# Self attention of a decoder layer: the probabilities of a head divided by their sums on ScalarE instead of GpSimd

## The chip, the cores and the metric
The kernel is one program on one core of a Trainium2 chip. The metric is the device time of one execution in microseconds, as the median of several. Engine names in the rows: PE is TensorE's matmul side and PEld its weight loads, DVE is VectorE, ACT is ScalarE, POOL is GpSimd, SP is SyncE.

## The reference
The program computes two decoder layers for 16 batches of 256 tokens of width 512, everything in float32. Its first step, the one that is changed here, is causal self attention with rotary positions:

```python
q = einsum('bsd,hdk->bshk', layernorm(x), W_Q) + b_Q      # 16 heads of 64; k and v alike
q, k = rotary(q), rotary(k)
scores = where(causal, einsum('bqhd,bkhd->bhqk', q, k) / 8, -inf)
pattern = softmax(scores, axis=-1)
x = x + einsum('bqhd,hdm->bqm', einsum('bhqk,bkhd->bqhd', pattern, v), W_O) + b_O
```

After it come a cross attention (`cross0`), an expert layer, a normalised linear attention (`norm`), a second cross attention (`cross1`) and an fp8 linear layer. Each is a phase of its own with a barrier behind it.

## The kernel before
`attention_phase` serves the self attention (`rotary` is true, tiles are called `self_...`) and both cross attentions (`rotary` is false, `cross_...`). A phase walks over 16 batches, and within a batch over 16 slots, one for each head. The five engines each run the same loop (`body(b, first, last)`) with their own part of every slot, and meet at semaphores. Each engine does its work in the order in which the code issues it, so the first thing that waits holds up all that is behind it on this engine.

For a head h of the self attention the steps are, in order:

1. TensorE, slot h (heads come in pairs, so in even slots): `scores` of h and h+1 into two of four banks, then the causal mask is added (L509, L516).
2. VectorE, `maxima` (L754): the negative row maxima of both heads of the pair. Four reductions of 128x128 and 128x256, one of each for a head.
3. ScalarE, `exps` in slot h (L617): exponentials from the bank into `prob`, two instructions (128x128 and 128x256), each with a reading of the accumulator that gives the row sums.
4. VectorE, `sums_inverse` in slot h+1 (L761): `rsum`, the reciprocals of the sums.
5. GpSimd (L404): `prob` times `rsum` in place, two instructions. It then raises `norm_ok`.
6. TensorE, `prob_transposes` in slot h+2 (L528): waits for `norm_ok` and transposes the probabilities into the bank `T`, which VectorE (even heads, L767) or ScalarE (odd heads, L625) copies to `probT`.
7. TensorE, `times_v` in slot h+4 (L544), into the bank `Z`; VectorE copies it to `zT` one slot later (`heads_done`, L776).

Between these steps stand the projections, by a fixed plan of slots (`PLAN`). Each goes through one of two banks `A`, used in turn: the use u waits until u-1 uses are free (`bank_for`).

- slots 0, 2, 4, 6, 8, 10, 12: `Q`, the transposes of the turned q and k of the next pair of heads (L456). ScalarE copies the q half (`self_QT`, L605), then VectorE the k half (`self_KT`, L699), which frees the bank
- slots 0 and 1, and 8 to 11, 14 and 15: `P`, projections of q and k, 12 matmuls each (L70 to L72). VectorE turns them (L827, L828), and GpSimd adds the two parts and the turned bias (L382, L384)
- slots 3 and 4: `O`, the output projection of the batch before, one half of the tokens each (L472). It needs all eight `zT` of that batch, the last of which VectorE writes in slot 3
- slots 5 and 6, and 12 and 13: `V`, projections of v, copied by VectorE (L694)
- slot 7: `X`, twice: transposes of the next batch's normalised x (L442); ScalarE rounds them to `self_xTh` (L598), VectorE takes the rest as `self_xTl` (L683)

`P` of slots 8 to 11, 14 and 15 belongs to the next batch. The first of them, in slot 8, and `Q` of slot 14 wait on TensorE until every earlier use of the two banks is free:

```python
if key in (("+", "P", 0, 0, 0), ("+", "Q", 0)):
    pe.wait_ge(a_free, u)
```

The orders of VectorE and ScalarE within a slot, which the argument needs:

- VectorE: `zT` of an earlier pair (odd slots), `maxima` of the pair (even slots), the copy of `probT` (even slots), `rsum` of head i-1, then the extras of the plan (`self_KT`, the turning, `self_xTl`, the copy of v)
- ScalarE: the copy of `probT` (odd slots), `exps` of head i, then the extras (`self_QT`, `self_xTh`)

Of the kernel before, what the change touches and what calls it, by code (L numbers as in the profile page):

```python
# [22 lines left out]
ALU = mybir.AluOpType  # L23
ACT = mybir.ActivationFunctionType
AX = mybir.AxisListType

P = 128
# [3 lines left out]
T = S // P  # L31
H = 16
# [43 lines left out]
def after(eng, sem, value):  # L76

    if not isinstance(value, int) or value > 0:
        eng.wait_ge(sem, value)


def over_rotated(eng, n, body, tail):


    body(0, True, False)
    if n > 2:
        with eng.Fori(1, n - 1) as b:
            body(b, False, False)
    body(n - 1, False, True)
    tail(n)  # L90
# [34 lines left out]
def attention_phase(nc, name, n_batch, x_in, x_out, consts, wq, wk, wv, wo,  # L125
                    d_head, causal, rotary, ctx=None, bq=None, bk=None, bv=None, bo=None, rope=None):
# [20 lines left out]
    KQ = [P * (t + 1) if causal else S for t in range(T)]  # L147
    SOFF = [sum(KQ[:t]) for t in range(T)]
# [4 lines left out]
    NP = 4 if rotary else 8  # L153
# [64 lines left out]
    with Phase(nc, name) as ph:  # L218
# [22 lines left out]
        rsum = ph.sb("rsum", [P, H, T])  # L241
        prob = ph.sb("prob", [P, NP, SW])
# [49 lines left out]
        rsum_ok = ph.sem("rsum_ok")  # L292
        norm_ok = ph.sem("norm_ok")
# [70 lines left out]
        @block.gpsimd  # L364
        def _(pool):
            def rstds(n):
                pool.wait_ge(ln, 7 * n + 5)
                pool.tensor_tensor(rstd[:, :], rstd[:, :], minus_half[:, :], ALU.pow).then_inc(ln_pow, 1)

            pool.memset(minus_half[:, :], -0.5).then_inc(pool_const, 1)  # L370
            pool.wait_ge(pool_const, 1)
            rstds(0)
            pool.wait_ge(const_in, 16 * N_CONST)
            if rotary:
                pool.wait_ge(rb_ok, 3 * 2 * T * CH)

            def turned(key, u, seq):

                _, which, c, t = key
                dst = (q_t, k_t)[which][:, t, c * 512:(c + 1) * 512]  # L380
                pool.wait_ge(a_free, u + 1)
                pool.tensor_tensor(dst, dst, turn[:, t % 2, :], ALU.add).then_inc(rot, 1)  # L382
                pool.wait_ge(rot, 2 * seq + 1)
                pool.tensor_tensor(dst, dst, rb[:, which, t, c * 512:(c + 1) * 512], ALU.add).then_inc(rot, 1)  # L384

            for key in BEFORE:
                if key[0] == "P":
                    turned(key, N_W + BEFORE.index(key), [k for k in BEFORE if k[0] == "P"].index(key))

            def body(b, first, last):  # L390
                seq = 0
                for i in range(H):
                    for key in PLAN[i]:
                        ahead = key[0] == "+"
                        if key[ahead] == "P" and not (ahead and last):
                            turned(key[ahead:], uses.at(key, b, first, last), P_BEFORE + b * P_PER + seq)
                            seq += 1
                    if i == STATS_AT and not last:
                        rstds(b + 1)

                    pool.wait_ge(rsum_ok, b * H + i + 1)
                    for t in range(T):
                        pr = prob[:, i % NP, SOFF[t]:SOFF[t] + KQ[t]]
                        ins = pool.tensor_tensor(pr, pr, rsum[:, i, t:t + 1].to_broadcast([P, KQ[t]]), ALU.mult)  # L404
                    ins.then_inc(norm_ok, 1)
                if bo is not None:

                    pool.wait_ge(res_in, b * 16 + 16)
                    for t in range(T):
                        pool.tensor_tensor(res[:, t, :], res[:, t, :], bo_r[:, :], ALU.add).then_inc(res_b, 1)  # L410
            over_rotated(pool, n_batch, body, lambda b: None)
# [166 lines left out]
        @block.scalar  # L578
        def _(act):
            if rotary:  # L580
                for i in range(N_STAGE):
                    w = (wqs, wks, wvs)[i // 2]
                    act.wait_ge(w_in[i % 3], 16 * KD * (i // 3 + 1))
                    act.activation(w[0][:, :, (i % 2) * 512:(i % 2 + 1) * 512],
                                   stage[i % 3][:, :, :].rearrange("p t n -> p (t n)").rearrange("p (k n) -> p k n", k=KD), ACT.Copy).then_inc(w_hi, 1)
            else:
                for u in range(N_W):
                    act.wait_ge(a_full, u + 1)
                    act.activation((wqs, wks, wvs, wos)[u // KD][0][:, u % KD, :], A[u % 2][:, :], ACT.Copy).then_inc(a_hi, 1)
            if not rotary and bq is not None:  # L590
                act.wait_ge(zeroed, 1)
            act.wait_ge(const_in, 16 * N_CONST)

            def extra(key, u, bank, n):
                if key[0] in "XC":
                    act.wait_ge(a_full, u + 1)
                    j = key[1]
                    act.activation((xT if key[0] == "X" else cT)[0][:, 2 * j:2 * j + 2, :].rearrange("p k n -> p (k n)"),  # L598
                                   A[bank][:, :], ACT.Copy).then_inc(a_hi, 1)
                elif key[0] == "Q":  # L600
                    g = key[1]
                    act.wait_ge(a_full, u + 1)
                    after(act, s_full, n * H + HPT * (g + 1 - n_qt))
                    if rotary or bq is None:
                        act.activation(QT[:, g % n_qt, :], A[bank][:, 0:S], ACT.Copy, scale=SCALE).then_inc(a_hi, 1)  # L605
                    else:

                        act.activation(QT[:, g % n_qt, :], A[bank][:, 0:S], ACT.Identity, bias=bq_c[:, g:g + 1], scale=SCALE).then_inc(a_hi, 1)

            for j, key in enumerate(BEFORE):  # L610
                extra(key, N_W + j, (N_W + j) % 2, 0)

            def exps(b, h):
                act.wait_ge(max_ok, b * H + h + 1)
                after(act, t_full, b * H + h - NP + 1)
                for t in range(T):
                    ins = act.activation(prob[:, h % NP, SOFF[t]:SOFF[t] + KQ[t]], SC[h % 4][:, SOFF[t]:SOFF[t] + KQ[t]], ACT.Exp,  # L617
                                         bias=neg_max[:, h, t:t + 1], scale=1.0, accum_out=sums[:, h, t:t + 1])
                ins.then_inc(exp_ok, 1)

            def probs_odd(b, h):
                if h % 2:
                    act.wait_ge(t_full, b * H + h + 1)
                    after(act, pv_ok, b * H + h - NPT + 1)
                    act.activation(probT[:, h % NPT, :], TP[:, 0:SW], ACT.Copy).then_inc(pt_odd, 1)  # L625

            def heads_hi(b, h, first, last):
                if not rotary and h % G == 0:
                    g = (h % H) // G
                    act.wait_ge(pv_ok, b * H + h + G)  # L630
                    if h == 0 and not first:
                        act.wait_ge(a_full, uses.at(("O", 1), b, first, last) + 1)
                    if bv is None:
                        act.activation(zTs[0][:, g, :], Z[:, 0:S], ACT.Copy).then_inc(z_hi, 1)
                    else:

                        act.activation(zTs[0][:, g, :], Z[:, 0:S], ACT.Identity, bias=bv_c[:, g:g + 1]).then_inc(z_hi, 1)

            def body(b, first, last):
                for i in range(H):  # L640
                    if not (first and i < Z_LAG):
                        heads_hi(b, i - Z_LAG, first, last)
                    if not (first and i < T_LAG):
                        probs_odd(b, i - T_LAG)
                    for j in EXP_AT[i % G]:
                        exps(b, i - i % G + j)
                    for key in PLAN[i]:
                        ahead = key[0] == "+"
                        if not (ahead and last) and key[ahead] in "QXC":
                            extra(key[ahead:], uses.at(key, b, first, last), uses.bank(key, b, first, last), b + 1 if ahead else b)  # L650

            def tail(b):
                for i in range(Z_LAG):
                    heads_hi(b, i - Z_LAG, False, False)
                    if i < T_LAG:
                        probs_odd(b, i - T_LAG)

            over_rotated(act, n_batch, body, tail)

# [1082 lines left out]
```

## Time and profile before

| | |
|---|---|
| median of 3 runs | 4279.06 us (4275.65 to 4281.77) |
| profiled execution | 4277.14 us, its span 4275.4 us |
| self attention | about 57 to 1400 us of the span |
| granted clock of TensorE over the span | 0.913 |
| busy over the span | PE 82%, PEld 57%, DVE 46%, POOL 33%, ACT 29% |
| POOL instructions of L404 on `self_prob` | 512, two for each of 256 heads |

How to read it: the span runs from the first to the last instruction of one profiled execution. The busy share of an engine is a mean over phases with different limits. A granted clock of 1.00 is TensorE at 2.4 GHz, 0.50 is 1.2 GHz, and a value between is a mean over the stretch. A row of busy time by stretch has, in order: the stretch in us from the span's start and its length; then for PE, PEld, DVE, ACT and POOL the busy time in us with the count of instructions; then the granted clock, the busy share of the DMA engines and GB/s. What stands in square brackets behind an instruction is the idle time of its engine before it and what ended that.

### The profile page before, as it was taken

The page shows a single profiled execution, that of the slowest core. Times are in us where ns is not written, and L with a number is a line of the kernel's source. Part 1 is how long each engine was busy: PE and PEld are TensorE (multiplying, and loading weights), DVE is VectorE, ACT ScalarE, POOL GpSimd, SP SyncE. Part 2 cuts the span into 40 slices and gives each one's busy share as a digit, 9 for nine tenths or more (in the row PEclk, how much of TensorE's full clock was granted, in tenths as well). Part 3 has the DMA queues.
Part 4 walks back from the last instruction along what each step waited for, and adds up shares of the span by engine and source line. Part 5 has one row for each costly group of instructions (what it writes and reads, how often), then busy time and mean ns, then how long its engine had stood idle before and what let it go on. Part 6 is the DMA issues. An engine that isn't in the chain of part 4 may idle for free. (4 is left out here: it accounts for less than half of the span.)

```text
span 4275.4 us, 70717 instructions
## 1 busy us (share of the span) xinstructions
PE 3514.4 (82%) x23116; PEld 2419.5 (57%) x23116; DVE 1965.1 (46%) x4934; ACT 1255.4 (29%) x4320; POOL 1421.7 (33%) x2092
## 2 busy tenths in 40 slices
PE   4999999999998799999857666655999799999955
PEld 3665666666565577777626111111777577777732
DVE  5444444444443455555450000001566466666657
ACT  2222222222222345555410000000111255555521
POOL 2444445444444133333310000000222145455437
PEclk9999999999998799999985877777999899999976
DMA  5000000000000211111166999997111211111113
GB/s 118 16 20 15 25 15 20 25 15 20 15 25 11 81 40 59 40 58 42 37 218 242 425 429 426 426 429 282 54 67 67 78 40 49 46 52 39 49 53 133
DMA packets 158787, 459.15 MB, mean 107 GB/s; under 512 B 47393, under 2 KB 51873, under 8 KB 138209
## 3 DMA queue, kind: packets, MB, share of 16 engines
q1 hardware_dynamic: 150272, 445.72, 27.3%
q10 hardware_dynamic: 8448, 12.59, 0.9%
q8 instruction: 36, 0.59, 0.1%
q14 instruction: 31, 0.25, 0.0%
HBM read 402.17 MB, written 56.10 MB: 107 GB/s over the span
## 5 line engine op out<-in xcount | busy, mean ns | idle before, releaser
L404 POOL TENSOR_TENSOR cross_prob<-cross_prob,cross_rsum 128x256 f32<-128x256 f32 (+1 forms) x1024 | 559.8, 572 | 760.9 <-DVE cross_rsum L761 760.9
L617 ACT ACTIVATE cross_prob<-cross_S,cross_neg_max 128x256 f32<-128x256 f32 (+1 forms) x1024 | 440.8, 464 | 1.4 <-DVE cross_neg_max L754 1.4
L617 ACT ACTIVATE self_prob<-self_S,self_neg_max 128x128 f32<-128x128 f32 (+1 forms) x512 | 210.2, 418 | 569.6 <-DVE self_neg_max L754 569.6
L404 POOL TENSOR_TENSOR self_prob<-self_prob,self_rsum 128x128 f32<-128x128 f32 (+1 forms) x512 | 247.8, 507 | 383.7 <-DVE self_rsum L761 383.3
L528 PE MATMUL cross_T<-cross_ident,cross_prob 128*128 128x128 f32 x1792 | 290.0, 279 | 85.6 <-ACT cross_probT L625 76.7
L528 PEld LDWEIGHTS cross_T<-cross_ident,cross_prob 128*128 128x128 f32 x1792 | 205.4, 142 | 147.4 <-issue 85.7
L1171 PE MATMUL experts_H<-moe_w,experts_tok 128*32 128x512 f32 x1024 | 167.8, 815 | 141.7 <-DMA moe_b<-in_L_ffn_w 137.2
L625 ACT ACTIVATE cross_probT<-cross_T 128x384 f32<-128x384 f32 (+1 forms) x256 | 139.7, 546 | 423.4 <-PE cross_T L528 423.4
L472 PE MATMUL self_A<-self_wo_f,self_zT 128*128 128x512 f32 x512 | 254.3, 656 | 0.6 <-DVE self_zT L776 0.6
L617 ACT ACTIVATION_READ_ACCUMULATOR cross_prob<-cross_S,cross_neg_max 128x1 f32 x1024 | 230.5, 225 | 0.0
L1189 PE MATMUL experts_O<-moe_w,experts_hidT 128*32 128x512 f32 x1024 | 170.1, 825 | 51.7 <-DMA moe_w<-in_L_ffn_w 45.9
L1311 POOL MEMSET norm_minus_half<- 128x2 f32 x1 | 0.1, 104 | 638.5 <-POOLq L53 638.5
L1231 DVE COPY experts_hidT<-experts_T 128x512 f32<-128x512 f32 x32 | 22.1, 691 | 381.9 <-PE experts_T L1182 381.9
L1171 PEld LDWEIGHTS experts_H<-moe_w,experts_tok 128*32 128x32 f32 x1024 | 44.5, 143 | 264.1 <-issue 257.7
L528 PE MATMUL self_T<-self_ident,self_prob 128*128 128x128 f32 x768 | 137.2, 290 | 59.2 <-POOL self_prob L404 58.1
L754 DVE TENSOR_REDUCE self_neg_max<-self_S 128x1 f32<-128x128 f32 (+1 forms) x512 | 147.1, 349 | 74.4 <-PE self_S L516 74.4
L756 DVE TENSOR_REDUCE cross_neg_max<-cross_S 128x2 f32<-128x512 f32 x256 | 158.9, 683 | 43.4 <-PE cross_S L509 43.3
L472 PEld LDWEIGHTS self_A<-self_wo_f,self_zT 128*128 128x128 f32 x512 | 107.0, 215 | 126.9 <-issue 125.9
L625 ACT ACTIVATE self_probT<-self_T 128x384 f32<-128x384 f32 x128 | 62.8, 490 | 344.9 <-PE self_T L528 344.9
L754 DVE TENSOR_REDUCE cross_neg_max<-cross_S 128x1 f32<-128x128 f32 (+1 forms) x512 | 141.3, 348 | 42.9 <-PE cross_S L516 42.9
L767 DVE COPY cross_probT<-cross_T 128x384 f32<-128x384 f32 (+1 forms) x256 | 156.1, 610 | 9.4 <-PE cross_T L528 9.4
L70 PE MATMUL cross_A<-cross_xTh,cross_wqh 128*128 128x256 f32 x512 | 156.1, 305 | 2.8 <-DVE cross_cTl L683 2.8
(270 smaller groups left out, 8896.3 us busy)
## 6 DMA issues: line engine op xcount, KB each, us to landing
moe_w<-in_L_ffn_w SPq DMA_DIRECT2D x64, 4096.0 KB, 34.9
cross_x_t<-x SPq DMA_DIRECT2D x32, 512.0 KB, 3.9
cross_c_t<-in_ctx SPq DMA_DIRECT2D x32, 512.0 KB, 4.8
cross_res<-x SPq DMA_DIRECT2D x32, 512.0 KB, 3.6
x<-cross_res SPq DMA_DIRECT2D x32, 512.0 KB, 2.8
self_x_t<-in_x SPq DMA_DIRECT2D x16, 512.0 KB, 3.6
self_res<-in_x SPq DMA_DIRECT2D x16, 512.0 KB, 3.6
x<-self_res SPq DMA_DIRECT2D x16, 512.0 KB, 2.8
```

Source lines behind the costliest of these rows:

```text
L70: pe.matmul(out, ah, bh, start=first, stop=False)
L404: ins = pool.tensor_tensor(pr, pr, rsum[:, i, t:t + 1].to_broadcast([P, KQ[t]]), ALU.mult)
L472: mm = pe.matmul(A[bank][:, :], zT[:, k, t * P:(t + 1) * P], wo_f[:, k, :], start=(k == 0), stop=(k == NT - 1))
L528: mm = pe.transpose(TP[:, o:o + P], prob[:, h % NP, SOFF[t] + k * P:SOFF[t] + (k + 1) * P], ident[:, :])
L617: ins = act.activation(prob[:, h % NP, SOFF[t]:SOFF[t] + KQ[t]], SC[h % 4][:, SOFF[t]:SOFF[t] + KQ[t]], ACT.Exp, bias=neg_max[:, h, t:t + ...
L625: act.activation(probT[:, h % NPT, :], TP[:, 0:SW], ACT.Copy).then_inc(pt_odd, 1)
L754: ins = dve.tensor_reduce(neg_max[:, h, t:t + 1], SC[h % 4][:, SOFF[t]:SOFF[t] + KQ[t]], AX.X, ALU.max, negate=True)
L756: ins = dve.tensor_reduce(neg_max[:, h, :], SC[h % 4][:, :].rearrange("p (t k) -> p t k", t=T), AX.X, ALU.max, negate=True)
L767: dve.tensor_copy(probT[:, h % NPT, :], TP[:, 0:SW]).then_inc(pt_even, 1)
L1171: pe.matmul(HP[s][32 * n:32 * n + 32, :], tok[:, s, k, :], w1_s[s][:, k, n * 512:(n + 1) * 512], start=(k == 0), stop=False, tile_position ...
L1189: mm = pe.matmul(OP[s][32 * n:32 * n + 32, :], hidT[:, s, q, 32 * n:32 * n + 32], w2_s[s][:, n, q, :], start=(q == 0), stop=(q == NQ - 1), ...
L1231: dve.tensor_copy(hidT[:, s, :, :].rearrange("p q n -> p (q n)"), TP[s][:, :]).then_inc(ht_ok, 1)
```

## The change
In the self attention the two multiplications by `rsum` go from GpSimd to ScalarE, as a copy with a scale for each row. ScalarE does them for head i-1 in slot i, after the exponentials of head i and ahead of the slot's extras. The cross attentions keep theirs on GpSimd. Nothing else is edited.

```diff
-                    pool.wait_ge(rsum_ok, b * H + i + 1)
-                    for t in range(T):
-                        pr = prob[:, i % NP, SOFF[t]:SOFF[t] + KQ[t]]
-                        ins = pool.tensor_tensor(pr, pr, rsum[:, i, t:t + 1].to_broadcast([P, KQ[t]]), ALU.mult)
-                    ins.then_inc(norm_ok, 1)
+                    if not rotary:
+                        pool.wait_ge(rsum_ok, b * H + i + 1)
+                        for t in range(T):
+                            pr = prob[:, i % NP, SOFF[t]:SOFF[t] + KQ[t]]
+                            ins = pool.tensor_tensor(pr, pr, rsum[:, i, t:t + 1].to_broadcast([P, KQ[t]]), ALU.mult)
+                        ins.then_inc(norm_ok, 1)
...
+            def normalised(b, h):
+
+                act.wait_ge(rsum_ok, b * H + h + 1)
+                for t in range(T):
+                    pr = prob[:, h % NP, SOFF[t]:SOFF[t] + KQ[t]]
+                    ins = act.activation(pr, pr, ACT.Copy, scale=rsum[:, h % H, t:t + 1])
+                ins.then_inc(norm_ok, 1)
...
                     for j in EXP_AT[i % G]:
                         exps(b, i - i % G + j)
+                    if rotary and not (first and i < 1):
+                        normalised(b, i - 1)
                     for key in PLAN[i]:
...
                     if i < T_LAG:
                         probs_odd(b, i - T_LAG)
+                    if rotary and i < 1:
+                        normalised(b, i - 1)
```

## Rows read from the trace of the kernel before

**Rows 1.** Busy time by stretch, the self attention (columns: see above).

```profile
57.00:1400.00 1343.00, 1228.37 (x6762) 834.02 (x6761) 616.49 (x1653) 332.93 (x1310) 617.85 (x815) 0.96 0.05 18
```

**Rows 2.** Waits by total, 200 to 1100 us: total, times, longest.

```profile
PE self_T L528 <- POOL self_prob L404: 33.6, 22, 2.6
...
PE self_A L456 <- DVE self_turn L828: 18.4, 11, 1.8
PE self_A L70 <- DVE self_KT L699: 16.1, 10, 1.6
...
PEld self_T L528 <- POOL self_prob L404: 10.1, 27, 0.7
```

**Rows 3.** Timeline of TensorE, slots 2 to 4: start, duration, instruction.

```profile
656.15 0.40 PE L516 MATMUL self_S<-self_mask_b,self_ident_b 128*128 128x128 bf16 x4
657.02 0.55 PE L528 MATMUL self_T<-self_ident,self_prob 128*128 128x128 f32 x3 [0.46 <-POOL self_prob L404]
...
657.62 0.38 PE L456 MATMUL self_A<-self_ident,self_k_t 128*128 128x128 f32 x2
660.59 0.54 PE L528 MATMUL self_T<-self_ident,self_prob 128*128 128x128 f32 x3 [2.59 <-POOL self_prob L404]
660.97 8.73 PE L472 MATMUL self_A<-self_wo_f,self_zT 128*128 128x512 f32 x16
...
672.29 7.03 PE L472 MATMUL self_A<-self_wo_f,self_zT 128*128 128x512 f32 x16
```

**Rows 4.** Timeline of GpSimd, slots 2 and 3.

```profile
659.49 1.90 POOL L404 TENSOR_TENSOR self_prob<-self_prob,self_rsum 128x128 f32<-128x128 f32 x4
```

**Rows 5.** The same columns in the wait of slot 3 and behind it.

```profile
657.00:660.50 3.50, 0.98 (x7) 0.75 (x7) 2.14 (x8) 1.21 (x5) 3.42 (x5) 1.00 0.00 0
...
662.00:664.00 2.00, 2.00 (x4) 0.72 (x3) 0.00 (x0) 0.46 (x3) 0.00 (x0) 0.50 0.00 0
```

**Rows 6.** The same columns after the waits of slots 8 and 14.

```profile
200.00:1100.00 900.00, 831.48 (x4605) 563.96 (x4604) 421.54 (x1132) 225.77 (x890) 422.30 (x556) 0.97 0.05 19
611.30:621.00 9.70, 9.65 (x57) 7.35 (x58) 4.63 (x12) 2.23 (x10) 5.29 (x7) 1.00 0.00 0
642.10:652.00 9.90, 9.89 (x63) 7.83 (x64) 4.70 (x13) 2.95 (x12) 7.88 (x9) 1.00 0.16 53
```

**Rows 7.** ScalarE's own durations: this op's nearest relatives.

```profile
L617 ACT ACTIVATE self_prob<-self_S,self_neg_max 128x256 f32<-128x256 f32 x174 | 81.9, 471 | 0.0
...
L617 ACT ACTIVATE self_prob<-self_S,self_neg_max 128x128 f32<-128x128 f32 x174 | 63.5, 365 | 394.7 <-DVE self_neg_max L754 394.7
...
L605 ACT ACTIVATE self_QT<-self_A 128x256 f32<-128x256 f32 x87 | 33.2, 381 | 45.0 <-PE self_A L456 45.0
```

**Rows 8.** By tile `top_pr`, duration min/median/max in ns: an ACTIVATE from SBUF to SBUF.

```profile
L1074 ACT ACTIVATE top_pr<-top_pr,top_nm x4: 491/492/507, 2233.1 to 2234.6; 128x256 f32<-128x256 f32 x4
```

**Rows 9.** Timeline of ScalarE, end of slot 7.

```profile
606.97 0.21 ACT L617 ACTIVATION_READ_ACCUMULATOR self_prob<-self_S,self_neg_max 128x1 f32 x1
607.07 1.09 ACT L598 ACTIVATE self_xTh<-self_A 128x512 fp32r<-128x512 f32 x2
```

**Rows 10.** Timeline of VectorE, slots 7 and 8.

```profile
607.70 1.29 DVE L683 TENSOR_TENSOR self_xTl<-self_A,self_xTh 128x512 fp32r<-128x512 f32 x2 [0.99 <-ACT self_xTh L598]
608.91 1.14 DVE L754 TENSOR_REDUCE self_neg_max<-self_S 128x1 f32<-128x128 f32 x4
...
610.43 0.15 DVE L761 RECIPROCAL self_rsum<-self_sums 128x2 f32<-128x2 f32 x1
610.77 0.42 DVE L699 COPY self_KT<-self_A 128x256 f32<-128x256 f32 x1 [0.19 <-ACT self_QT L605]
```

**Rows 11.** TensorE in slot 8, at the first projection for the next batch.

```profile
611.33 0.49 PE L70 MATMUL self_A<-self_wqh,self_xTh 128*128 128x512 f32 x1 [1.61 <-DVE self_KT L699]
```

**Rows 12.** Timeline of VectorE, slots 2 and 3.

```profile
656.48 1.15 DVE L754 TENSOR_REDUCE self_neg_max<-self_S 128x1 f32<-128x128 f32 x4 [0.49 <-PE self_S L516]
...
658.45 0.42 DVE L699 COPY self_KT<-self_A 128x256 f32<-128x256 f32 x1
658.79 0.47 DVE L776 TENSOR_SCALAR self_zT<-self_Z,self_bv_c 128x256 f32<-128x256 f32 x1
```

## The prediction, made before the changed kernel was run

> **What bounds the kernel now.** I first read the busy time by stretch, to find which engine fills the self attention. TensorE is busy for 1228.37 of 1343 us, ScalarE for 332.93, GpSimd for 617.85 [rows 1]. So the phase is bound by TensorE, and what another engine does costs time only where TensorE stands still for it, or where its clock falls.
>
> Then the waits by total over 11 of the 16 batches [rows 2]. TensorE's transposes waited 33.6 us for GpSimd's product, 3.05 us a batch. Two other waits stand beside it: 18.4 us for the turning (1.66 us a batch, slot 14), and 16.1 us for `self_KT` (slot 8, 1.61 us each time [rows 11]).
>
> The timeline shows where the 3.05 us are. Slot 2 waits 0.46 us and slot 3 2.59 us [rows 3]: GpSimd still adds up the q and k of the projections, and gets to the products of heads 1 and 2 only at 659.49 [rows 4], though the sums of head 1 were there earlier. Behind the wait of slot 3 the granted clock is 0.50 in 662 to 664 us, the lower of the two levels, 1.2 GHz [rows 5]. What TensorE did before: 0.98 us of work in 3.5 us [rows 5]. The 16 matmuls of `O` that fall into it take 8.73 us, and the same 16 one slot later 7.03 us [rows 3]: 1.70 us lost a visit. Behind the waits of 1.61 us (slot 8) and 1.66 us (slot 14) the clock stayed at 1.00, 2.4 GHz [rows 6]. Over the 11 batches it was 0.97 [rows 6]; 3% of 900 us is 27 us, 2.4 us a batch, about that one visit, sometimes a longer one.
>
> **What the change removes.** 512 GpSimd products go. GpSimd was on the path only in the waits named: 3.05 us a batch at TensorE, and part of the 10.1 us that weight loads waited [rows 2]. That is 0.92 us a batch, most of it the same wait of slot 2; the rest, in later slots, I take as 0.3 us, between nothing and 0.46. The projections' additions on GpSimd come a little earlier; nobody waits for them for long.
>
> **What it adds.** Two ScalarE instructions a head, SBUF to SBUF, with a scale read for each row. No row shows this one. The nearest: an ACTIVATE of 128x256 in SBUF with a bias for each row takes 0.492 us [rows 8]; from a PSUM bank 0.471, and its 128x128 form 0.365 [rows 7]. So 0.49 and 0.39 us. Neighbours overlap by 0.11 us (606.97 + 0.21 against 607.07 [rows 9]), say 0.10. The pair takes 0.78 us, and what is behind it starts 0.68 us later. Bounds: without the row operand 0.381 for the large one [rows 7], pair about 0.65; at no overlap 0.88.
>
> The Trainium skill (VectorE: DVE Perf Modes, section "The TRN2 errata — SBUF-src ops pay a fixed extra latency per instruction") speaks against moving this work here: ScalarE pays 224 cycles of fixed cost from SBUF and 172 from PSUM, an estimated 0.04 us more for each instruction. Here 0.492 against 0.471 shows half of that [rows 7, 8]; by the page the sum below would be 1 to 2 us longer.
>
> ScalarE is idle most of the time, so by busy share 512 more instructions are free. By order they are not: they stand ahead of the slot's extras. I follow each place where an extra is waited for.
>
> Slot 7: the pair of head 6 stands between the exponentials of head 7 and the two roundings of x, which start at 607.07 [rows 9] as soon as ScalarE is free. They come 0.68 us later, and with them the two subtractions of VectorE, behind which stand the maxima of slot 8, at 608.91 back to back [rows 10]. They start at 609.59.
>
> Slot 8: `rsum` comes 1.52 us behind the start of the maxima (610.43 - 608.91 [rows 10]), since VectorE copies a transposed head between them. Until now `self_QT` did not wait for it. Now it waits for the pair, and the pair for `rsum`: 609.59 + 1.52 + 0.15 for `rsum` + 0.08 for the signal = 611.34, then 0.68 to `self_QT` (612.02), 0.41 to `self_KT` (612.43), and 0.56 from the start of `self_KT` to TensorE, as before (611.33 - 610.77 [rows 10, 11]). TensorE starts the projection at 612.99 where it was 611.33: **+1.66 us**, a wait of 3.27 us where it was 1.61.
>
> Slots 2 and 3: the maxima start at 656.48, after a wait for TensorE, so nothing earlier moves them [rows 12]. `rsum` of head 1 is done at 658.15, the pair runs 658.23 to 659.01, and head 1's transposes start at 659.07, not 660.59 [rows 3]. But `self_KT` also moves, from 658.45 to 658.23 + 0.68 + 0.41 = 659.32, and the last `zT` is behind it on VectorE, 0.34 us later: 659.66 to 660.13 [rows 12]. The output projection needs it. It starts at 660.23, not 660.97 [rows 3]: **-0.74 us**, though the transposes come 1.5 us earlier.
>
> Other even slots: `self_KT` comes 1.0 us later too (1.86 us behind the start of the maxima before [rows 10], 2.84 now). What TensorE does next there is a projection of 12 matmuls, about 3 us, so it is hidden; with the least to spare in slot 6. If that cover were gone, the two transposes of x would start late.
>
> **Sum.** A batch: +1.66 - 0.74 - 0.3 = +0.62 us; 15 batches, +9.3 us. The first and last batch have few projections, and there heads wait for GpSimd's products as well: some -2 us. Bounds of the pair: it counts twice in slot 8 and once in slot 3, so 0.13 us less gives 6 us less, 0.1 us more 5 us more.
>
> **The clock.** It now costs about 2.2 to 2.4 us a batch. The wait of slot 3 is cut into 1.5 us (657.62 + 0.38 less the shift of slot 2, to 659.07) and 0.8 us, which is less than what brought the lower level down and more than what did not; I expect it in a part of the batches. The wait of slot 8 becomes longer than the 2.59 us that brought it in this row's batch; I expect it there in most. One visit costs 1.7 us. So the loss moves and stays about as large; I put -1 us for it. 4277.1 + 9.3 - 2 - 1 = 4283.4 for the profiled execution, which stands 1.9 us below the median: 4285.3, say **4286 us**.
>
> **Rivals.**
>
> - The forecast: the stall moves from slot 3 to slot 8, the clock's loss with it. Own range 4274 to 4300. Chance 0.62.
> - Slower by more: the lower level comes in slot 8 and in slots 2 and 3 as well. For: both waits lie above the 1.66 us that were harmless [rows 2, 6]. Against: the second is broken up. 15 visits of 1.7 us or a little more are 26 to 30 us: 4313. It decides if the two shorter waits of slots 2 and 3 count together as the one long wait did. Chance 0.15.
> - Faster: the lower level comes in neither place. For: no single wait of slots 2 and 3 is now over 1.7 us. Against: slot 8's 3.3 us. Then 15 x 2.3 = 34 us come back against 9.3 - 2: 4252. Chance 0.15.
> - Much faster: the pair is covered in slots 7 and 8, and all of the 3.05 + 0.3 us and the clock come back: 15 x 5.6 = 84 us, 4195. Against: ScalarE's roundings start back to back and the maxima too [rows 9, 10]. Chance 0.05.
> - The rest 0.03.
>
> **How the numbers follow.** Within 0.2% is 8.6 us, about what this kernel's measurement can tell. The forecast lies at +7, so of its 0.62 I give 0.35 to no change, 0.25 to slower, 0.02 to faster. With 0.15 slower, 0.15 + 0.05 faster and the rest: faster 0.22, same 0.37, slower 0.41. The range 4256 to 4312 takes in the forecast's own and goes to both clock rivals.
>
> **What would show it.** In the waits: TensorE's wait of slot 8 for `self_KT` at 3.2 us instead of 1.61; transposes of slot 3 that wait 1.4 us for ScalarE, then 0.8 us of the output projection for `zT`; no wait for GpSimd left in this phase. The pair at 0.39 and 0.49 us. The clock at 0.50 behind slot 8. The prediction is wrong in its order if slot 7's maxima chain does not move, and in its size if the clock does not follow the waits as said.

## The result, and the profile after

The changed kernel takes 4299.55 us in the median, the one before 4275.65 us beside it: ratio 1.0054, 95% interval 1.0032 to 1.0077. It is slower, by 24 us or 0.5%. In the profiled executions the difference is 27.6 us (4304.70 against 4277.14), and all of it arises in the self attention. The last instruction of that phase that VectorE does ends 27.5 us later. First the kernel before, then the changed one:

```profile
1403.30 0.69 DVE L709 TENSOR_TENSOR self_res<-self_A,self_res 128x512 f32<-128x512 f32 x1 [6.17 <-PE self_A L472]
```

```profile
1430.82 0.69 DVE L722 TENSOR_TENSOR self_res<-self_A,self_res 128x512 f32<-128x512 f32 x1 [6.18 <-PE self_A L473]
```

Busy time by stretch of the changed kernel, the self attention (columns as in [rows 1]):

```profile
57.00:1400.00 1343.00, 1226.57 (x6686) 845.26 (x6685) 608.94 (x1635) 518.34 (x1794) 378.71 (x303) 0.94 0.05 18
```

GpSimd has lost 239 us of work against [rows 1], ScalarE has gained 185. Neither bounds the phase. The granted clock went from 0.96 to 0.94. The waits of the changed kernel by total, 200 to 1100 us, beside [rows 2]:

```profile
PE self_A L70 <- DVE self_KT L712: 34.9, 11, 3.2
...
PE self_A L457 <- DVE self_turn L841: 18.3, 11, 1.7
PE self_T L529 <- ACT self_prob L633: 18.1, 10, 1.8
...
PE self_A L473 <- DVE self_zT L789: 4.9, 10, 0.6
```

TensorE waits for GpSimd no more in this phase. The wait of slot 8 has doubled, from 1.61 to 3.17 us a batch. In slots 2 and 3 there are now 1.81 us for ScalarE and then up to 0.6 us for `zT`, where there were 0.46 and 2.59 us. Timeline of TensorE, slots 2 and 3 of two batches:

```profile
416.42 0.49 PE L529 MATMUL self_T<-self_ident,self_prob 128*128 128x128 f32 x3
...
419.16 0.54 PE L529 MATMUL self_T<-self_ident,self_prob 128*128 128x128 f32 x3 [1.81 <-ACT self_prob L633]
420.28 7.13 PE L473 MATMUL self_A<-self_wo_f,self_zT 128*128 128x512 f32 x16 [0.58 <-DVE self_zT L789]
...
504.27 8.37 PE L473 MATMUL self_A<-self_wo_f,self_zT 128*128 128x512 f32 x16 [0.40 <-DVE self_zT L789]
```

VectorE in the same slots, beside [rows 12]:

```profile
416.51 1.15 DVE L767 TENSOR_REDUCE self_neg_max<-self_S 128x1 f32<-128x128 f32 x4 [0.49 <-PE self_S L517]
...
419.33 0.42 DVE L712 COPY self_KT<-self_A 128x256 f32<-128x256 f32 x1 [1.13 <-ACT self_QT L606]
419.67 0.47 DVE L789 TENSOR_SCALAR self_zT<-self_Z,self_bv_c 128x256 f32<-128x256 f32 x1
```

From the start of the maxima to the output projection are 3.77 us (420.28 - 416.51); before they were 4.49 (660.97 - 656.48 [rows 3, 12]). That is 0.72 us won, though the transposes of head 1 alone come 1.46 us earlier (2.65 us behind the maxima, not 4.11). `self_KT` starts 2.82 us behind the maxima, not 1.97, and holds up the last `zT`.

Slot 8. ScalarE at the end of slot 7, then VectorE, then TensorE:

```profile
447.17 0.21 ACT L618 ACTIVATION_READ_ACCUMULATOR self_prob<-self_S,self_neg_max 128x1 f32 x1
447.26 0.80 ACT L633 ACTIVATE self_prob<-self_prob,self_rsum 128x128 f32<-128x128 f32 x2
447.95 1.08 ACT L599 ACTIVATE self_xTh<-self_A 128x512 fp32r<-128x512 f32 x2
```

```profile
449.78 1.14 DVE L767 TENSOR_REDUCE self_neg_max<-self_S 128x1 f32<-128x128 f32 x4
...
451.31 0.15 DVE L774 RECIPROCAL self_rsum<-self_sums 128x2 f32<-128x2 f32 x1
452.59 0.42 DVE L712 COPY self_KT<-self_A 128x256 f32<-128x256 f32 x1 [1.13 <-ACT self_QT L606]
```

```profile
453.15 0.79 PE L70 MATMUL self_A<-self_wqh,self_xTh 128*128 128x512 f32 x1 [3.17 <-DVE self_KT L712]
...
538.38 0.79 PE L70 MATMUL self_A<-self_wqh,self_xTh 128*128 128x512 f32 x1 [3.17 <-DVE self_KT L712]
```

The pair stands between the accumulator's reading and the roundings of x, which follow 0.69 us after its start. `self_KT` starts 2.81 us behind the maxima, not 1.86 [rows 10]. The first matmul behind the wait takes 0.79 us, not 0.49 [rows 11]: the clock is down. Busy time by stretch of the changed kernel, behind slot 3 of one batch, behind slot 8, and ahead of slot 3 of the next batch:

```profile
504.00:506.50 2.50, 2.23 (x3) 1.18 (x4) 0.21 (x2) 1.89 (x7) 0.00 (x0) 0.50 0.00 0
538.50:544.00 5.50, 5.50 (x14) 4.23 (x15) 0.00 (x0) 0.00 (x0) 0.00 (x0) 0.50 0.00 0
571.00:588.00 17.00, 15.22 (x100) 11.47 (x100) 9.19 (x25) 7.75 (x28) 12.74 (x10) 1.00 0.09 31
```

The lower level, 1.2 GHz, comes twice in this batch, and behind slot 8 it lasts more than 5.5 us. In what follows, one such stretch is called a visit; in all the traces here a visit in the steady batches lasts either about 3.4 or about 6.8 us. Last, ScalarE's own durations by form, for the instruction that no row of before showed:

```profile
L633 ACT ACTIVATE self_prob<-self_prob,self_rsum 128x256 f32<-128x256 f32 x170 | 85.0, 500 | 0.0
...
L633 ACT ACTIVATE self_prob<-self_prob,self_rsum 128x128 f32<-128x128 f32 x170 | 68.7, 404 | 17.7 <-DVE self_rsum L774 12.9
```

### The profile page after: what moved, and what is told of

The parts are those of the page before. It is cut to its first block and busy times, and to the rows that moved or that the text cites. A ratio compares the mean times of both kernels' runs of the same rounds, so it can differ in the third digit from the quotient of the medians.

```text
span 4302.9 us, 70507 instructions
## 1 busy us (share of the span) xinstructions
PE 3538.2 (82%) x23116; PEld 2442.2 (57%) x23116; DVE 1964.0 (46%) x4934; ACT 1449.2 (34%) x4832; POOL 1182.5 (27%) x1580
## 5 line engine op out<-in xcount | busy, mean ns | idle before, releaser
L382 POOL TENSOR_TENSOR self_q_t<-self_q_t,self_turn 128x512 f32<-128x512 f32 x64 | 81.7, 1277 | 718.4 <-DVE self_turn L841 718.3
L473 PE MATMUL self_A<-self_wo_f,self_zT 128*128 128x512 f32 x512 | 245.0, 634 | 8.0 <-DVE self_zT L789 8.0
L633 ACT ACTIVATE self_prob<-self_prob,self_rsum 128x128 f32<-128x128 f32 (+1 forms) x512 | 205.4, 452 | 27.6 <-DVE self_rsum L774 21.3
L70 PE MATMUL self_A<-self_wqh,self_xTh 128*128 128x512 f32 x256 | 123.4, 482 | 83.9 <-DVE self_KT L712 47.4
```

The costliest lines, as they stand in the source:

```text
L70: pe.matmul(out, ah, bh, start=first, stop=False)
L473: mm = pe.matmul(A[bank][:, :], zT[:, k, t * P:(t + 1) * P], wo_f[:, k, :], start=(k == 0), stop=(k == NT - 1))
L633: ins = act.activation(pr, pr, ACT.Copy, scale=rsum[:, h % H, t:t + 1])
```

## The experiments

All ratios are to the kernel before, with 95% intervals. The changed kernel stands at 1.0054.

**The division behind the extras, everywhere** (extras_first). "The division" is the pair of multiplications by `rsum`. In ScalarE's loop:

```diff
-                    if rotary and not (first and i < 1):
-                        normalised(b, i - 1)
                     for key in PLAN[i]:
...
+                    if rotary and not (first and i < 1):
+                        normalised(b, i - 1)
```

> The changed kernel, with ScalarE's division of head i-1 behind the slot's extras (self_QT, self_xTh) and no longer ahead of them; all else as changed. Theory A (order): the 512 instructions cost nothing in themselves, what they cost is that two chains stand behind them. So the wait of slot 8 goes from 3.17 us back to 1.61 us, head 1's transposes still start about 1.4 us earlier than before the change, and the output projection right behind them. Against the kernel before: -1.4 - 0.3 us a batch for the waits, and some 2 us a batch of clock if neither wait brings the lower level; 15 batches, about -55 us, ratio 0.987. Theory B (load): 512 more instructions (some 205 us busy) on ScalarE slow the chain of exponentials wherever they stand: the time stays within 0.3% of the changed kernel, ratio 1.003 to 1.008. Theory C (clock only): the changed kernel is slower since the clock falls more often; the waits do not matter by themselves: ratio about 1.00, with the clock up.

Ratio 0.9969 (0.9959 to 0.9979), 4262.49 us. Faster than both kernels, so theory B falls: the 512 instructions are still there. But it missed theory A's 0.987 widely and lies nearer to the 1.00 of theory C, the clock. Half of TensorE's busy time at the lower level in the self attention, an estimate of what that level costs, fell from 71 us in the changed kernel to 34 us, of 47 us between the two profiled executions. TensorE's waits by total show where it still stands:

```profile
PE self_T L529 <- ACT self_prob L633: 35.4, 22, 1.9
...
PE self_A L457 <- DVE self_turn L844: 18.3, 11, 1.7
...
PE self_A L70 <- DVE self_KT L715: 15.9, 11, 1.5
```

Slot 8 is back at 1.45 us. But TensorE now waits for ScalarE 22 times in this stretch, not 10 times. The second is in slot 15, behind the wait of slot 14. TensorE, then ScalarE:

```profile
468.63 0.43 PE L457 MATMUL self_A<-self_ident,self_q_t 128*128 128x128 f32 x2 [1.66 <-DVE self_turn L844]
468.90 0.38 PE L457 MATMUL self_A<-self_ident,self_k_t 128*128 128x128 f32 x2
470.61 0.90 PE L529 MATMUL self_T<-self_ident,self_prob 128*128 128x128 f32 x3 [1.33 <-ACT self_prob L633]
```

```profile
469.42 0.38 ACT L606 ACTIVATE self_QT<-self_A 128x256 f32<-128x256 f32 x1 [4.08 <-PE self_A L457]
469.70 0.79 ACT L633 ACTIVATE self_prob<-self_prob,self_rsum 128x128 f32<-128x128 f32 x2
```

In slot 14 ScalarE stood 4.08 us before `self_QT`, with the division of head 13 behind it. The transposes then take 0.90 us, not 0.50. Waits of 1.66 and 1.33 us with 0.65 us of work between them were followed by the lower level in all 14 batches that have them; 1.66 us alone was not, in any run.

**The same, but in slot 14 ahead of the extras** (behind_not14).

```diff
+                    late = i != 14
+                    if rotary and not late and not (first and i < 1):
+                        normalised(b, i - 1)
                     for key in PLAN[i]:
...
+                    if rotary and late and not (first and i < 1):
+                        normalised(b, i - 1)
```

> As extras_first, but in slot 14 the division stands ahead of the extras again. There the extra (self_QT of Q) waits for TensorE until late in the slot, and in extras_first the division of head 13 waited behind it and TensorE's transposes for 1.33 us. Theory A (order): that wait goes; slots 3, 8 and 14 each keep one wait of 1.4 to 1.9 us and none of them brings the lower level. Against the kernel before: -1.5 us a batch of waits, -2.2 us of clock, 15 batches: -55 us, ratio 0.987. Theory B (load of ScalarE): no more than extras_first, ratio 0.997.

Ratio 0.9878 (0.9861 to 0.9895), 4224.84 us, as expected. Slots 2 to 4 on TensorE; both halves of the output projection now take 7.03 us, with nothing between transposes and projection:

```profile
398.07 0.54 PE L529 MATMUL self_T<-self_ident,self_prob 128*128 128x128 f32 x3 [1.89 <-ACT self_prob L633]
398.45 7.03 PE L473 MATMUL self_A<-self_wo_f,self_zT 128*128 128x512 f32 x16
...
408.08 7.03 PE L473 MATMUL self_A<-self_wo_f,self_zT 128*128 128x512 f32 x16
```

**Slot 8's wait for `self_KT` taken away**, in the changed kernel (nowait_after), in the one before (nowait_before), and in the one just shown (behind_not14_nowait). The projection has its own bank, and the rest of x is in the uses that `bank_for` waits for.

```diff
-                        if key in (("+", "P", 0, 0, 0), ("+", "Q", 0)):
+                        if key in ((("+", "Q", 0),) if rotary else (("+", "P", 0, 0, 0), ("+", "Q", 0))):
                             pe.wait_ge(a_free, u)
```

> The changed kernel, in which the first projection for the next batch (slot 8) no longer waits until self_KT has freed its bank, but only for its own bank and for the rest of x. Theory A (the stall sits at this wait): 3.17 us a batch of waiting and the lower clock level behind it (6.8 us of it in most batches, 3.4 us lost) go; 15 batches x 6.5 us = -95 us against the changed kernel, ratio to the kernel before 0.98 to 0.985. Theory B (ScalarE's chain holds everything up): the wait comes back at the next thing that needs self_KT or head 7's transposes, and less than 1.5 us a batch is won, ratio 1.000 to 1.003.

> The kernel before the change, with the same wait of slot 8 taken away. 1.61 us a batch and no clock loss go: 15 batches, -24 us, ratio 0.9944, if the clock behind slot 3 stays as it was. Beside the same edit of the changed kernel it says what the change is worth where slot 8 does not stop TensorE: theory A wants the changed one then faster than this one by some 45 us (0.74 + 0.3 us a batch of waits and up to 2.2 us of clock); theory B wants it slower still.

> behind_not14 without slot 8's wait for self_KT. Theory A: another 1.5 us a batch of waiting, 15 batches, -22 us: ratio 0.982, some 15 us ahead of nowait_after. If ScalarE's load were the limit, no faster than nowait_after, 0.985.

The changed kernel falls to 0.9854 (0.9838 to 0.9870), 4214.12 us: 85 us less than with the wait, near the expected 95. The kernel before falls to 0.9960 (0.9945 to 0.9974), 4259.62 us, 16 us and not 24. Its granted clock is lower, 0.96 over 200 to 1100 us instead of 0.97 [rows 6]: the wait of slot 3 is the same, but every visit behind it now lasts 6.8 us, where most lasted 3.4 us.

```profile
200.00:1100.00 900.00, 847.37 (x4662) 573.66 (x4661) 425.86 (x1143) 229.86 (x901) 424.94 (x561) 0.96 0.05 19
```

So where slot 8 does not stop TensorE, the change is worth 45 us (4259.62 - 4214.12), just what theory A said: where the exposed chain is absent, moving the products from GpSimd to ScalarE is a gain. Most of it is clock. By the same estimate the lower level costs 57 us without the change and 23 us with it. The third kernel takes 4199.12 us, ratio 0.9816 (0.9797 to 0.9834), the fastest of all.

**The clock by itself.** Eight matmuls whose result is overwritten, ahead of TensorE's wait: in the changed kernel in slot 8 (fill8_after), in the kernel before in slot 3 (fill3_before). The edit in slot 8:

```diff
+                        if key == ("+", "P", 0, 0, 0) and rotary:
+                            bank_for(u)
+                            for _ in range(8):
+                                pe.matmul(A[uses.bank(key, b, first, last)][:, :], xT[0][:, 0, 0:P], wqs[0][:, 0, 0:512], start=True, stop=True)
```

> The changed kernel with 8 matmuls of 128x512 added, whose result is overwritten, between the transposes of slot 8 and its wait for self_KT (some 1.9 us of TensorE work in a wait of 3.17 us). They shorten no chain. Theory C (most of the loss beyond the waits is the clock): the granted clock stays at 1.00 behind slot 8, 3.4 us a batch come back, 15 batches, -50 us against the changed kernel, ratio to the kernel before about 0.993. If the time goes with the waits alone, nothing changes: ratio 1.005.

> The kernel before the change, with 8 matmuls of 128x512 added whose result is overwritten, on TensorE ahead of its wait for GpSimd in slot 3 (1.9 us of work in a wait of 2.59 us). No chain is shorter. Theory C (clock): the lower level behind slot 3 goes, 2.2 us a batch: -33 us, ratio 0.992. If the clock were not what those matmuls lose by, nothing changes: ratio 1.00.

The changed kernel: 0.9978 (0.9968 to 0.9987), 4264.15 us, 35 us less (32 by the two ratios), with 8 x 15 more matmuls. Expected were 50 us and a ratio of 0.993, so it fell short: the visits behind slot 8 are gone, but in slot 3, where nothing was filled, the lower level still comes in 8 of 14 batches. The added work takes 2.12 us, the projection still waits for `self_KT`, and its first matmul takes 0.50 us and no longer 0.79:

```profile
437.80 2.12 PE L567 MATMUL self_A<-self_wqh,self_xTh 128*128 128x512 f32 x8
440.95 0.50 PE L70 MATMUL self_A<-self_wqh,self_xTh 128*128 128x512 f32 x1 [1.03 <-DVE self_KT L716]
```

In the kernel before the added work takes 2.11 us. Its ratio is 0.9930 (0.9913 to 0.9947), 4245.49 us against 4276.73 us beside it, 31 us less. The output projection of slot 3 takes 7.03 us and not 8.73 [rows 3], and the clock over 200 to 1100 us is 1.00:

```profile
407.26 0.54 PE L528 MATMUL self_T<-self_ident,self_prob 128*128 128x128 f32 x3 [0.75 <-POOL self_prob L404]
407.64 7.03 PE L472 MATMUL self_A<-self_wo_f,self_zT 128*128 128x512 f32 x16
```

```profile
200.00:1100.00 900.00, 850.13 (x4817) 584.71 (x4815) 433.21 (x1161) 232.90 (x917) 433.58 (x570) 1.00 0.06 19
```

**The division behind the extras in one slot only**: 7, 8 or 2.

```diff
+                    late = i in (7,)
```

> The changed kernel with the division behind the extras in slot 7 alone. Theory A: of the 1.56 us by which the wait of slot 8 has grown, the pair of slot 7 is 0.68: the wait falls from 3.17 to 2.5 us, the rest stays. 15 batches x 0.68 = -10 us, and the clock may fall less often, up to 2 us a batch: between -10 and -40 us against the changed kernel, ratio 0.996 to 1.003. Rival: VectorE's copies, not the pair of slot 7, set the start of the maxima, and the wait stays 3.17 us, ratio 1.005.

> The changed kernel with the division behind the extras in slot 8 alone. Theory A: this is the other part of slot 8's grown wait, 1.56 - 0.77 (measured in slot7_behind) = 0.8 to 0.95 us: the wait falls from 3.17 to 2.2 to 2.4 us, and with it the longer visits to the lower level (6.8 us become 3.4, as in slot7_behind): ratio about 1.000. If the two parts did not add up, the wait would stay over 2.7 us.

> The changed kernel with the division behind the extras in slot 2 alone. Theory A: the output projection no longer waits 0.58 us for the last zT, the transposes ahead of it wait 0.1 us more: -0.5 us a batch, -7 us, with the stall of 3.17 us in slot 8 as in the changed kernel. With the 0.58 us gone, the clock no longer falls in slot 3 either, in half or more of the batches (in behind_not14 a single wait of 1.9 us rarely brought the lower level), 1.7 us a visit: ratio 0.997 to 1.003. Rival: another thing than self_KT holds the zT up, and the 0.58 us stay, ratio 1.005.

| division behind in | ratio | median us | wait of slot 8 | wait for `zT` |
|---|---|---|---|---|
| nowhere (changed kernel) | 1.0054 (1.0032 to 1.0077) | 4299.55 | 3.17 | up to 0.6 |
| slot 7 | 1.0008 (0.9999 to 1.0018) | 4277.93 | 2.40 | 0.58 |
| slot 8 | 0.9970 (0.9959 to 0.9980) | 4262.04 | 2.22 | 0.58 |
| slot 2 | 0.9970 (0.9958 to 0.9981) | 4264.11 | 3.17 | none |

The last two columns are in us. The two parts of slot 8's growth are 0.77 us (slot 7) and 0.95 us (slot 8). Together 1.72 us, more than the 1.56 us by which the wait had grown: with the division behind everywhere it is 1.45 us, less than the 1.61 us of before; why it is less stays open. Slot 8's edit did better than its expected 1.000, since the level also fell less often in slot 3, which that edit does not touch. The wait for `zT` goes with the pair of slot 2. Both rivals fall. The times, though, do not follow the waits: slot 2's edit takes 0.5 us a batch of waiting away (the transposes wait 1.89 us, not 1.81) and wins 35 us, 2.4 us a batch. The rest is clock. Busy time by stretch over 200 to 1100 us in slot2_behind, granted clock 0.98, then in the changed kernel, 0.95:

```profile
200.00:1100.00 900.00, 825.84 (x4663) 571.59 (x4662) 425.56 (x1144) 362.14 (x1254) 260.68 (x209) 0.98 0.06 19
```

```profile
200.00:1100.00 900.00, 825.23 (x4510) 568.78 (x4510) 411.27 (x1103) 349.63 (x1209) 260.04 (x208) 0.95 0.05 18
```

## Why the prediction came out as it did

The forecast was 4286 us, with 0.41 on slower, 0.37 on no change and 0.22 on faster. Measured: 4299.55 us, slower, inside the range of 4256 to 4312 and at the very end of the forecast's own 4274 to 4300; the profiled execution, 4304.70 us, lies beyond that. The order of the waits was understood, and slower was the likeliest of the three by a little. Most of the measured slowing, though, is a clock term that the sum had wrong; that the time still fell inside the range is owed to a width that took in the clock rivals.

- **That the stall moves from slot 3 to slot 8** was right, shown by the traces and by the kernels without slot 8's wait. The wait there was to be 3.27 us, and is 3.17. Its two parts were 0.68 and 0.98 us; undone one at a time they measure 0.77 and 0.95.
- **That slots 2 and 3 give back only 0.74 us** was right: 0.72. `self_KT` and with it the last `zT` hold the projection up, which slot2_behind confirms.
- **The pair at 0.78 us** measures 0.80, its parts 0.404 and 0.500 us, foreseen 0.39 and 0.49. The larger one stands 0.03 us above the exponential of the same shape out of PSUM, 0.471 us [rows 7]. For a source in SBUF, the Trainium skill (VectorE: DVE Perf Modes, section "The TRN2 errata — SBUF-src ops pay a fixed extra latency per instruction") gives 52 more fixed cycles, an estimated 0.04 us. The sign agrees; the two instructions here also differ in their function, so the 0.03 us is not the source's alone.
- **The cover in the other even slots** held: no further wait of TensorE appeared.
- **The clock term failed in size and sign.** I had put -1 us: the loss moves and stays as large. The waits account for +1.56 - 0.72 - 0.3 = +0.54 us a batch, 8 us in 15 batches, less the 2 us of the ends. The profiled difference is 27.6 us, so by this sum some 21 us are the clock. It may be all of it: the same estimate from the two traces gives 44 us before and 71 us after. The 0.3 us for later slots was never measured alone and would then be larger. The rival that had the lower level in both places (0.15, 4313 us) is what the trace shows: 0.50 behind slot 3 and behind slot 8 in one batch, and behind slot 8 for longer than one of the old visits. The filled waits price it: 31 us were lost to slot 3's wait before, and 35 us are lost to slot 8's wait now, with slot 3's on top.
- **The step under that term**: the prediction cut the wait of slot 3 into 1.5 and 0.8 us and expected the level there in a part of the batches only. The pieces are 1.81 and 0.58 us, and the level came in 12 of 14 batches. The first piece is longer because TensorE is done with slot 2 0.68 us earlier (0.84 us behind the start of the maxima, 417.35 - 416.51, not 1.52), and not only 0.46. So the first piece alone already lies above the 1.66 us that had been harmless.
- **The second, short wait is not shown to be the cause.** In 10 of the 12 batches it is shorter, 0.40 or 0.46 us, because the level had already fallen while the transposes ran, ahead of it. The stretch of the transposes at 503.16, before and behind the fall:

```profile
503.00:503.35 0.35, 0.19 (x2) 0.20 (x3) 0.02 (x1) 0.29 (x2) 0.00 (x0) 1.00 0.00 0
503.45:503.85 0.40, 0.40 (x3) 0.03 (x1) 0.40 (x2) 0.00 (x0) 0.00 (x0) 0.50 0.00 0
```

- **The same two waits without the lower level** stand in slot8_behind, where it came behind them in 1 of 14 batches:

```profile
653.42 0.55 PE L529 MATMUL self_T<-self_ident,self_prob 128*128 128x128 f32 x3 [1.80 <-ACT self_prob L633]
654.54 7.13 PE L473 MATMUL self_A<-self_wo_f,self_zT 128*128 128x512 f32 x16 [0.57 <-DVE self_zT L792]
```

- **What the runs leave open**: what, beside the waits, decides a batch. One undivided wait of 1.89 us was followed by the level in none of the 14 batches (extras_first and slot2_behind alike), in 4 (behind_not14) and in 6 (behind_not14_nowait).
- **The gain is real but was spent.** The same change is worth 45 us where slot 8 does not wait, and 52 us (4276.73 - 4224.84) once the extras go ahead of the division in every slot but 14.

## What to carry to other kernels

Work moved to an idle engine costs by its place in that engine's order: put it behind what others wait for and ahead of what itself waits long, slot by slot: the first rule alone won 13 us over the kernel before, and with slot 14 excepted 52 us. Before moving work, look for the one wait on TensorE that needs more than it must: with slot 8's wait gone the same edit gained 45 us, with it the edit lost 24. And do not price a TensorE wait by its length alone. Slot 14's 1.66 us cost no clock until 1.33 us followed 0.65 us of work later, and one and the same pair of waits in slot 3 brought the lower level in 12 of 14 batches of one kernel and in 1 of 14 of another.

## What the hardware showed that I had not expected

- The same waits, another clock. Waits of 1.61 and 1.66 us never brought the lower level, 2.59 and 3.17 us did in every batch. Between them it varied with the kernel: 1.81 us, 0.5 to 0.7 us of work and then up to 0.58 us brought it in 1 (slot8_behind), 5 (slot7_behind and nowait_after), 8 (fill8_after) and 12 (the changed kernel) of 14 batches.
- The visit's length varied as well. Behind the same 3.17 us in slot 8 it lasted 6.8 us in 12 of 14 batches of the changed kernel, and 3.4 us in all 14 of slot2_behind.
- Useless matmuls in a wait make the kernel faster: 8 of them a batch, 2.1 us of work in a wait, won 31 us and 35 us.
- Three kernels with different waits in slot 8 (1.45, 2.22 and 3.17 us) came out within 2.1 us of each other (4262.49, 4262.04 and 4264.11). Most of this is no riddle: TensorE's waits of a batch in slots 3, 8, 14 and 15 add up to 6.33, 6.26 and 6.72 us, and in nearly every batch each kernel has one visit, of 3.4 us. In all three the same instruction returns 81.9 us later in the next batch; in the changed kernel 85.2 us later (538.38 - 453.15). Why these distances are the ones that last was not tried and stays open.

The three in this order, extras_first, slot8_behind and slot2_behind, at slot 8 of two batches each:

```profile
438.33 0.49 PE L70 MATMUL self_A<-self_wqh,self_xTh 128*128 128x512 f32 x1 [1.44 <-DVE self_KT L715]
...
520.24 0.49 PE L70 MATMUL self_A<-self_wqh,self_xTh 128*128 128x512 f32 x1 [1.45 <-DVE self_KT L715]
```

```profile
440.71 0.79 PE L70 MATMUL self_A<-self_wqh,self_xTh 128*128 128x512 f32 x1 [2.22 <-DVE self_KT L715]
...
522.64 0.79 PE L70 MATMUL self_A<-self_wqh,self_xTh 128*128 128x512 f32 x1 [2.22 <-DVE self_KT L715]
```

```profile
442.70 0.79 PE L70 MATMUL self_A<-self_wqh,self_xTh 128*128 128x512 f32 x1 [3.17 <-DVE self_KT L715]
...
524.63 0.79 PE L70 MATMUL self_A<-self_wqh,self_xTh 128*128 128x512 f32 x1 [3.17 <-DVE self_KT L715]
```
